# Local transformer: values projected per tile and read back in blocks of 64 keys, in place of merged value and output weights

## The reference

```python
qkv = x @ Wqkv
q, k, v = jnp.split(qkv, 3, -1)
q = l2norm(q) * qs;  k = l2norm(k) * ksc      # then rotary with xpos scale
out = local_attention(q, k, v)                # per window of 32 queries
out = out.transpose(0, 2, 1, 3).reshape(b, n, INNER)
return out @ Wo
...
def local_attention(q, k, v):                 # w = 32
    bk2, bv2 = look(bk), look(bv)             # 64 keys: window before and own
    sim = einsum('bhwie,bhwje->bhwij', bq, bk2) * QK_SCALE
    sim = where(mask, -max, sim)
    attn = softmax(sim, -1)
    return einsum('bhwij,bhwje->bhwie', attn, bv2)
```

## Time and profile before

| | us |
|---|---|
| three runs, median (lowest, highest) | 5540.9 (5526.91, 5541.35) |
| profiled execution: span from first to last instruction | 5525.2 |
| TensorE busy in it | 4705.2 |
| VectorE busy | 3719.1 |
| ScalarE busy | 2827.0 |
| GpSimd busy | 2810.2 |
| local transformer stage, first to last projection | 220 to 3567 |
| a step of the loop, by kind (0, 1, 2, 3), most often | 20.3, 17.8, 14.5, 15.4 |

### The profile page before, as it was taken

How to read it: one execution, slowest core, us unless ns; L and a number is a source line. 1 busy time by engine, 2 the same in 40 slices (tenths; PEclk the granted TensorE clock), 3 DMA queues, 4 the chain that set the end, 5 groups by cost and what they waited for, 6 DMA issues and landing times. The chain is left out here.

```text
span 5525.2 us, 143465 instructions
## 1 busy us (share of the span) xinstructions
PE 4705.2 (85%) x57069; PEld 3341.4 (60%) x57103; DVE 3719.1 (67%) x8589; ACT 2827.0 (51%) x6227; POOL 2810.2 (51%) x3349
## 2 busy tenths in 40 slices
PE   7699999999999999999999999954375999945886
PEld 3366666666666666666666666633263666623665
DVE  7677777777777777777777677748724656667442
ACT  2266565666666656666666656631022666641332
POOL 4477666777677667766777667601022333311000
PEclk9899999999999999999999999977587999967897
DMA  0211111111111111111111110000211000010002
GB/s 21 70 29 25 25 34 35 25 25 34 36 25 25 31 31 29 25 34 31 28 24 34 25 24 20 17 24 2 67 50 32 2 2 1 1 24 13 26 29 56
DMA packets 312162, 150.60 MB, mean 27 GB/s; under 512 B 146143, under 2 KB 301003, under 8 KB 311243
## 3 DMA queue, kind: packets, MB, share of 16 engines
q1 hardware_dynamic: 309451, 137.20, 10.3%
q0 software_dynamic: 2048, 4.20, 0.3%
HBM read 101.10 MB, written 27.41 MB: 23 GB/s over the span
## 5 line engine op out<-in xcount | busy, mean ns | idle before, releaser
L1435 POOL TENSOR_TENSOR loc_a<-loc_a,loc_b 128x512 f32<-128x512 f32 x768 | 976.9, 1274 | 234.0 <-DVE loc_b L1511 233.5
L1123 PE MATMUL psum<-loc_wqk,loc_xt 128*128 128x512 f32 x1536 | 828.9, 622 | 15.3 <-issue 4.7
L1186 PE MATMUL psum<-loc_m,xn_rows 128*128 128x128 f32 x6144 | 823.7, 277 | 4.8 <-DVE y_rows L1543 3.0
L1307 ACT ACTIVATE loc_sq<-psum 128x512 f32<-128x512 f32 x768 | 455.1, 593 | 682.6 <-PE psum L1123 681.3
L1460 POOL TENSOR_TENSOR loc_a<-loc_a,loc_rn 128x512 f32<-128x512 f32 x768 | 785.4, 1045 | 0.1
L1186 PEld LDWEIGHTS psum<-loc_m,xn_rows 128*128 128x128 f32 x6144 | 754.3, 193 | 48.2 <-issue 45.5
L1507 DVE TENSOR_TENSOR loc_a<-psum,loc_rope 128x512 f32<-128x512 f32 x768 | 523.2, 681 | 332.4 <-ACT loc_sq L1307 318.3
L1467 POOL TENSOR_TENSOR xn_cols<-xn_cols,loc_rec 128x512 f32<-128x512 f32 x384 | 394.1, 1047 | 685.3 <-DVE loc_rec L1538 684.9
L1344 ACT COPY xn_rows<-psum 128x512 f32<-128x512 f32 x768 | 411.7, 588 | 219.6 <-PE psum L1174 215.9
L1511 DVE TENSOR_TENSOR loc_b<-psum,loc_rope 128x512 f32<-128x512 f32 x768 | 520.5, 678 | 0.0
L1515 DVE TENSOR_REDUCE loc_n<-loc_sq 128x8 f32<-128x512 f32 x768 | 516.9, 673 | 0.0
(11 more groups left out here) (372 smaller groups left out, 8565.0 us busy)
## 6 DMA issues: line engine op xcount, KB each, us to landing
loc_x<-loc_shifted SPq DMA_DIRECT2D x192, 256.0 KB, 4.0
loc_shifted<-y_rows SPq DMA_DIRECT2D x144, 64.0 KB
loc_wqk<-in_L_ffn_Wqkv SPq DMA_DIRECT2D x24, 256.0 KB, 3.7
x_rows<-y_rows SPq DMA_DIRECT2D x96, 64.0 KB
x_rows<-y_rows SPq DMA_DIRECT2D x96, 63.5 KB
moe_w<-in_L_ffn_W SPq DMA_DIRECT2D x16, 256.0 KB, 4.7
l3a_qk<-l3a_rot SPq DMA_DIRECT2D x16, 256.0 KB, 2.1
grp_w<-in_L_ffn_W SPq DMA_DIRECT2D x16, 256.0 KB, 4.2
```

The source lines that it names most:

```text
L1123: nc.tensor.matmul(ring("p", i, unit), xt[:, b % 2, t * P:(t + 1) * P], wqk[:, unit * 512:(unit + 1) * 512], start=True, stop=True).then_i ...
L1186: last = nc.tensor.matmul(y_bank[:, 0:P], u[:, i % 2, h // 2, h % 2, :], m[:, h, :], start=(h == 0), stop=(h == HEADS - 1))
L1307: nc.scalar.activation(sq[:, g % 2, :], ring("p", i, unit), ACT.Square).then_inc(sem["squared"], 1)
L1435: nc.gpsimd.tensor_tensor(part, part, b_[:, g % 2, :], ALU.add).then_inc(sem["added"], 1)
```

## The change

Values are made after all and the merged weights go. In step n `project_values(n, h)` multiplies the tile's input by half of Wv (the even or the odd heads, 512 columns), twice, in the places of two of the four parts of `project_out`; each result takes a slot of the ring, which now has six tiles a step. `copy_values` on ScalarE puts it into SBUF, `keep_values` writes the tile's 128 rows of 1024 values (512 KB) to memory, and one step later `load_windows` reads 64 keys x 4 windows x 512 values for each half of the heads (two transfers of 512 KB a tile). `mix` makes 64 small products per tile in one block: 64 keys x 64 features of one head as weights, 32 queries streamed, on the four quarters of the array. Two copies follow in place of four, and `project_out` needs only 8 matmuls, two heads stacked to 128 rows, in two parts.

```diff
-                def mix(i, piece):
+                def project_values(i, h):
                     b, t = i // TPB, i % TPB
+                    if i % NT == 0:
+                        pe.wait_ge(wv_in[h], 16 * (i // NT + 1))
+                    wait_ring(pe, "v", i, h)
+                    nc.tensor.matmul(ring("v", i, h), xt[:, b % 2, t * P:(t + 1) * P], wv[:, h, :], start=True,
+                                     stop=True).then_inc(sem["v_done"], 1)
+
+                def mix(i):
                     pe.wait_ge(sem["copied"], copied_at["p", i, 1])
-                    for v in range(2):
-                        w = 2 * piece + v
-                        for h in range(2):
-                            rows_h = slice(64 * h, 64 * h + 64)
-                            last = nc.tensor.matmul(u_bank[h][:, 256 * v:256 * v + 256], x2[rows_h, b % 3, WPT * t + w, :],
-                                                    pt[rows_h, i % 2, :, 32 * w:32 * w + 32], start=True, stop=True, skip_group_check=True)
+                    pe.wait_ge(v2_in[i % 3], 32 * (i // 3 + 1))
+                    if i >= 1:
+                        pe.wait_ge(sem["u_copied"], 2 * i)
+                    for q in range(PAIRS // 2):
+                        for w in range(WPT):
+                            at = q * P + WINDOW * w
+                            for c in range(2):
+                                j = 2 * q + c
+                                for h in range(2):
+                                    rows_h = slice(64 * h, 64 * h + 64)
+                                    last = nc.tensor.matmul(u_bank[h][64 * c:64 * c + 64, at:at + WINDOW], v2[rows_h, i % 3, w, j * DH:(j + 1) * DH],
+                                                            pt[rows_h, i % 2, j, WINDOW * w:WINDOW * (w + 1)], start=True, stop=True,
+                                                            skip_group_check=True)
...
-                    for h in range(4 * part, 4 * part + 4):
-                        last = nc.tensor.matmul(y_bank[:, 0:P], u[:, i % 2, h // 2, h % 2, :], m[:, h, :], start=(h == 0),
-                                                stop=(h == HEADS - 1))
+                    for j in range(4 * part, 4 * part + 4):
+                        last = nc.tensor.matmul(y_bank[:, 0:P], u[:, i % 2, j, :], wo[:, l % 2, j, :], start=(j == 0), stop=(j == PAIRS - 1))
...
+                add_ring(("p", n, 0), "rotated", UNITS * n + 1)
+                add_ring(("p", n, 1), "rotated", UNITS * n + 2)
+                add_ring(("v", n, 0), "v_copied", 2 * n + 1)
+                add_ring(("p", n, 2), "rotated", UNITS * n + 3)
+                add_ring(("p", n, 3), "rotated", UNITS * n + 4)
+                add_ring(("v", n, 1), "v_copied", 2 * n + 2)
```

```diff
+                def keep_values(i):
+                    b, t = i // TPB, i % TPB
+                    sp.wait_ge(sem["v_copied"], 2 * (i + 1))
...
                 for n in range(LAST_STEP):
-                    q = group_at(n, 14)
-                    if q is not None and q // PER_LAYER + 1 < LAYERS:
-                        keep_group(q // PER_LAYER + 1, q % PER_LAYER)
-                    if n % 2 == 1 and n + 1 < TILES:
-                        load_windows((n + 1) // 2)
+                    if 0 <= n - 1 < TILES:
+                        load_windows(n - 1)
+                    if n < TILES:
+                        keep_values(n)
                     if n % 2 == 0 and 0 <= (n - 6) // 2 < BATCHES:
                         shift_rows((n - 6) // 2)
```

More of the change, by code:

```diff
@@ L38 @@
 QK_SCALE = 8.0
+VALUE_SLOTS = 3
 NE, DFF = 8, 512
@@ new lines, in load_windows @@
+                def load_windows(i):
+                    b, t = i // TPB, i % TPB
+                    if t > 0:
+                        sp.wait_ge(v_kept[(i - 1) % 2], 16 * ((i - 1) // 2 + 1))
+                    sp.wait_ge(v_kept[i % 2], 16 * (i // 2 + 1))
+                    if i >= 3:
+                        sp.wait_ge(sem["u_done"], i - 2)
+                    for h in range(2):
+                        first = core.values[b % VALUE_SLOTS, t * P, h * PAIRS * DH]
+                        src = bass.AP(core.values.tensor, first.offset, [[INNER, 2 * WINDOW], [WINDOW * INNER, WPT], [1, PAIRS * DH]])
+                        sp.dma_start(v2[64 * h:64 * h + 64, i % 3, :, :], src).then_inc(v2_in[i % 3], 16)
@@ L1199, in multiply_weights @@
-                def multiply_weights(l):
-                    pe.wait_ge(sem["v_copied"], 2 * (l + 1))
-                    for half in range(2):
-                        for h in range(2):
-                            wait_ring(pe, "w", l, 2 * half + h)
-                        for j in range(4 * half, 4 * half + 4):
-                            for h in range(2):
-                                rows_h = slice(64 * h, 64 * h + 64)
-                                last = nc.tensor.matmul(ring("w", l, 2 * half + h)[:, j % 4 * P:(j % 4 + 1) * P], wvt[rows_h, j, :],
-                                                        wo[rows_h, j, :], start=True, stop=True, skip_group_check=True)
-                        last.then_inc(sem["m_done"], 1)
@@ L1266, in _ @@
                         turn_probs(n - 3, 1)
-                    if now(4):
-                        project_out(n - 4, 2)
+                    if now(0):
+                        project_values(n, 1)
                     if group_at(n, 11) is not None:
                         turn_rows(group_at(n, 11))
-                    for half in range(2):
-                        if starts(n, 1 + half) is not None:
-                            turn_values(n // NT, half)
                     if now(3):
-                        mix(n - 3, 0)
+                        mix(n - 3)
                     if group_at(n, 12) is not None:
@@ L1409, in _ @@
                         copy_rows(group_at(n, 11))
-                    for half in range(2):
-                        if starts(n, 1 + half) is not None:
-                            copy_values(n // NT, half)
                     if now(3):
@@ L1613, in _ @@
                         store_group(group_at(n, 13))
-        for clear in (zero, zero_wqk, zero_rope, zero_in, zero_kept, zero_x2, zero_xs):
+        for clear in (zero, zero_wqk, zero_rope, zero_wv, zero_wo, zero_in, zero_kept, zero_v2, zero_xs):
             clear()
```

146 lines of the change are left out of this document (59 added, 87 removed).

## The result

| | us |
|---|---|
| before, median (lowest, highest) | 5535.4 (5526.9, 5541.4) |
| after, median (lowest, highest) | 5647.0 (5645.5, 5663.1) |
| ratio, with its 95% interval | 1.0215 (1.0197 to 1.0232) |
| profiled span before, after | 5525.2, 5661.2 |

The changed kernel is 112 us slower, by the profiled spans 136 us: the profiled execution of the kernel before is its fastest, that of the changed kernel its slowest (5663.1; the other three take 5645.5 to 5648.1). The forecast was 27 us faster, and the range ended at 5625. The direction was wrong, and the time lies just under the upper end of rival 3 (5650).

What follows compares the result with a forecast made beforehand. TensorE's own instruction sequence was taken as the bound. Mix -52, merged weights -34, hidden layer -8, PSUM ring +25, instruction supply +30, layer boundary +10, pipe filling +2 sum to -27 us: 5540.9 to 5514, range 5445 to 5625.

Steps and rivals of the forecast that it cites:

- rival 3: Mix as forecast, supply gaps double, VectorE's wait whole: +23 us, 5564; chance 0.22 within 0.3%, 0.13 beyond, up to 5650.
- The mix: TensorE's new block of 64 small matmuls: 1.95 us against 2.22 before, -0.27 us per tile, -52 us in all.
- Rival 2: Mix block slower, each quarter loading and then multiplying: 2.75 us, total +92, about 5633 us; chance 0.15.
- The other savings: On TensorE: output product -1.92 and value projection +1.92 us per tile cancel; merged weights gone -34 us; hidden layer -8 us.
- kinds 0 to 3: Four kinds of TensorE loop step in turn, some with feed-forward parts; forecast about 19.8, 17.5, 14.2, 15.4 to 15.8 us.
- The hidden layer's wait: Hidden layer's second part waits for a GELU behind two mix copies, one afterwards: -8 us (0 to -17).
- PSUM ring: Six tiles instead of four per step through two banks; projection 2 waits for VectorE once in four steps: +25 us.
- The layer's boundary: Next layer's query weights, issued later behind the 0.5 MB write, come about 2 us late, five times: +10 us (0 to 30).
- Instruction supply: Issue gaps in TensorE's dense blocks grow as the mix adds 256 records 4 us after the scores: +30 us (0 to 150).
- Transfers: Value writes and window reads per tile: hidden, with 25 us of cover before the mix needs the rows.
- The two signs named for a wrong forecast: The mix waiting for its value windows, or TensorE's busy share in the stage falling below 90%.
- the forecast's merged weights: Once a layer, 8 transposes and 16 products on TensorE disappear: 5.6 us times 6, -34 us.

Runs made afterwards that it cites:

- e1: Changed kernel with all its DMAs, but each write carries 64 of 1024 columns and each read 32 of 512: 5547.2 us, ratio 1.0025.
- e10: Changed kernel with the value-window read issued behind the mix and, in a layer's last step, the next layer's weights ahead of it: 5580.1 us, ratio 1.0097.
- e2: Kernel before plus an unused 0.5 MB write and 1 MB read per tile: 5728.0 us, ratio 1.0362.
- e6: Changed kernel with full 0.5 MB writes, but reads of only 32 of 512 columns: 5553.0 us, ratio 1.0045.
- e4: Kernel before with the scores cut into four blocks, other work between them: 5647.5 us, ratio 1.0210.
- e9: Changed kernel with reads behind the mix, scores in two blocks, next layer's weights ahead of the read, row normalisation behind rotations of units 0 and 1: 5480.5 us, ratio 0.9918.

## Why the prediction was wrong

**The mix: right.** 1.95 us were forecast; in the timeline of an earlier step of the changed kernel,

```profile
2167.33 2.07 PE L1194 MATMUL psum<-xn_cols,loc_v 64*64 64x32 f32 x128
2169.33 0.44 PE L1124 MATMUL psum<-ident,y_rows 128*128 128x128 f32 x2
```

it takes 2169.33 - 2167.33 = 2.00, or 15.6 ns a record. Rival 2's 2.75 us are not seen, and 2.00 is also the median of the 162 mix blocks without a gap inside. Loads and matmuls of one half of the rows, 64 each, would take over 5 us one after another by the prediction's estimates (55 and 27 ns), so loads do hide, also under matmuls of quarters that share their rows. The rule of the Trainium skill, "TensorE: Matmul & The Clock Gate", section "Part 3: Packing small matmuls" (a load overlaps only where the row group differs), does not hold for this block, as far as these estimates go; taken strictly it would have given the 5 us, not the 2.75 that the prediction put down to it. The floor of about 25 ns from start to start, in Part 2 of the same page of the Trainium skill, is not seen either: 15.6 ns a record.

**The other savings: right.** Output product and value projection cancel. The shortest steps of each kind once the pipeline is full, first projection to first projection, are 19.6, 17.0, 14.1 and 15.8 us, against the forecast 19.8, 17.5, 14.2 and 15.4 to 15.8 (kinds 0 to 3). Their means are 21.5, 17.7, 15.2 and 19.2, and what lies between is for the most part the gaps and the clock: kinds 3 and 0 have 29 of the 30 long gaps. The merged weights are gone. The hidden layer's wait of 17.4 us for the GELU is gone, twice the 8 that were taken (the 0.9 us for the turned rows are as before).

**PSUM ring: right in size**, 16.6 + 8.9 = 25.5 us against 25. It was put at projection 2, and most of it (16.6, all in the steps of kind 3) stands at the first value projection, ahead of it: that one needs unit 0 rotated behind the normalised rows.

**The layer's boundary: right.** Of L1134's issue waits, 9.8 us, 7.6 stand at a layer's first projection, 2.3 to 2.6 us in three of five layers; 10 were forecast.

**Instruction supply: the step that failed.** It was given +30 us, with 150 as the bound. It measured +142 of gaps (8 of them the boundary's), and the clock after them, which had no term, up to 66 us more ((160 - 27) / 2). Density alone, in e1, is +83 of gaps. The step held that the mix, at 15 ns a record, would seldom starve; it starves little itself (32 us), but it uses up what would have been in store for the next scores, whose gaps rise from 75 to 121 us in e1; that last link is my reading of the two numbers, not shown by itself. The value taken was near the lower bound, where the rows gave no reason for it: the matmul records of the program had grown by a third (57069 to 76063), and the block with 71 us of gaps was already at the edge.

**Transfers: the same mistake from the other side.** The step asked whether the mix would wait for its windows. It never does. It did not ask what else uses the DMA engines: the instruction packets do, as the runs bear out, and in a third of the steps the read is issued under 7 us ahead of the one block that needs a packet in time. That was named only as the tail of rival 3, with a chance of 0.13 and its end at 5650, and this is the rival that came nearest: gaps of the scores and the mix together are 201 us, over the 150 that were its sign. The bytes have cost 100 us (e1), 67 of which are its place (e10). The two signs named for a wrong forecast did not show: the mix never waits for its windows, and TensorE is busy for 92% of the stage, not under 90%.

The sum with measured sizes, by spans: mix -42, hidden layer -17, ring +25, gaps with the boundary +142, clock up to +66; with the forecast's merged weights, -34, and start, +2, which were not measured by themselves: up to +142, against 136 measured.

## What to carry to other kernels

When a block already shows "issue" gaps, its engine lives at the edge of its instruction supply: count the records that a change adds to the same step, and treat every large DMA issued within some 7 us ahead of that block as competing with it, even if its data are wanted much later. Before a good change is given up, try where its transfers are issued and whether dense blocks can be cut: here three changes of order and one cut took the changed kernel from 2.2% slower to 0.8% faster. A cut has a price of its own: whatever the moved piece is put ahead of comes later, here a projection for which VectorE and then the exponentials wait. Where these have room the price is not asked, so the same cut can lose 1.3% in one kernel and gain 1.0% or more in the other.

## What the runs showed of the hardware that was not expected

- A 1 MB read under a dense block stretched the issue gaps of the scores from at most 2.1 us to 5.5 us (6.1 in e2); 0.5 MB writes at a quieter place did not (e6). That packets queue on the same DMA engines is inferred from when they start and from the place of the read; the way in which they queue was not measured.
- After a long gap TensorE ran at 1.2 GHz: in the timeline above for 5 us after 5.55 us of idling. Over the stage 160 us passed at the lower clock, against 27 before.
- Each cut of the dense f32 block cost some 0.08 us in the scores ((1.62 - 1.39) / 3) and up to 0.12 us in a block between (e4), while removing all gaps.
- Still open: whether the nearer place of the read is the whole reason why the transfers cost 195 us in the kernel before and 100 in the changed one, and why the issue gaps come back in e9.
